# A gated cross-attention block with a spiking FFN on one core: the first batches' steps in another order, roundings moved to ScalarE, smaller gate groups

## What is computed

```python
q = layernorm(x); k = v = ctx                    # 8 heads of 32
ig, fg = gates(concat(q, k, v))                  # per token and head
cs = cumsum(log_sigmoid(fg)); log_D = masked(cs_i - cs_j + ig_j)
C = (q @ k.T / sqrt(32)) * exp(log_D - rowmax(log_D))
h = (C / max(|C.sum|, exp(-rowmax))) @ v
x1 = x + tanh(g0) * layernorm(h) * ln_scale
y = square(relu(layernorm(x1) @ W_fc.T)) @ W_proj.T       # 256 -> 1024 -> 256
n = number of spikes of y in 5 leaky integrate-and-fire steps
out = x1 + tanh(g1) * n / 5
```

## Time and profile before

| | us |
|---|---|
| median of 3 runs (lowest, highest) | 690.0 (688.1, 690.67) |
| the profiled execution | 687.64 |
| its span, first to last instruction | 685.8 |
| PE busy | 616.9 |
| DVE busy | 523.9 |
| ACT busy | 400.4 |
| POOL busy | 323.9 |

### The profile page before, as it was taken

The page is one execution under the profiler, slowest core; times in us unless marked ns, Lnnn a source line. Parts: engine busy times, 40 slices in busy tenths (PEclk is TensorE's granted clock), DMA queues, the critical chain, the costliest instruction groups (busy, mean ns, idle before and its releaser), DMA issues.

```text
span 685.8 us, 17089 instructions
## 1 busy us (share of the span) xinstructions
PE 616.9 (90%) x6064; PEld 523.6 (76%) x6064; DVE 523.9 (76%) x1218; ACT 400.4 (58%) x863; POOL 323.9 (47%) x391
## 2 busy tenths in 40 slices
PE   2355688899999999999999999999999999999975
PEld 1245677778887888888888888888888878787865
DVE  4768687897888878897979878887888696948242
ACT  4654464765747756665756674775667464644432
POOL 3566657563555274544675365527454445510000
PEclk9999899999999999999999999999999999999998
DMA  8863677674429437752692657562774065000000
GB/s 242 157 150 76 133 127 127 125 129 104 82 86 199 74 104 140 142 89 91 129 173 65 117 112 158 96 108 96 138 144 73 24 126 95 15 18 32 0 32 31
DMA packets 73171, 71.29 MB, mean 104 GB/s; under 512 B 8704, under 2 KB 68736, under 8 KB 73088
## 3 DMA queue, kind: packets, MB, share of 16 engines
q1 hardware_dynamic: 71968, 70.02, 50.2%
q10 hardware_dynamic: 1120, 0.18, 0.1%
HBM read 27.44 MB, written 8.39 MB: 52 GB/s over the span
## 4 chain that ended last, share of the span: by engine, by line
PE 75%; DVE 8%; issue 7%; ACT 4%; POOL 3%; DMA 2%; SPq 1%; DVEq 0%; POOLq 0%; ACTq 0%
PE y_ps L1007 28%; PE z_ps L971 24%; PE misc_ps L448 4%; PE qk_ps L695 4%; PE arg_ps L680 3%; PE misc_ps L514 2%; PE pv_ps L742 2%; PE pv_ps L744 2%; PE pv_ps L743 2%; PE pv_ps L819 2%; DVE pv_ps L871 1%; DVE decay L714 1%; DVE stat L345 1%; ACT relu L981 1%; ACT decay L706 1%
## 5 line engine op out<-in xcount | busy, mean ns | idle before, releaser
L724 POOL TENSOR_TENSOR c_lo<-decay 128x512 bf16<-128x512 f32 x128 | 132.7, 1042 | 153.9 <-DVE decay L714 153.7
L1007 PE MATMUL y_ps<-wpr,relu 128*128 128x256 f32 x680 | 160.8, 381 | 1.2 <-issue 1.2
L1007 PEld LDWEIGHTS y_ps<-wpr,relu 128*128 128x128 f32 x680 | 124.9, 190 | 17.2 <-issue 1.4
L971 PE MATMUL z_ps<-x_hi,wfc_hi 128*128 128x512 f32 (+1 forms) x288 | 124.9, 434 | 5.9 <-ACT relu L981 3.8
L706 ACT ACTIVATE decay<-arg_ps,lqk_col 128x512 f32<-128x512 f32 x128 | 87.3, 682 | 37.5 <-PE arg_ps L683 31.3
L971 PE MATMUL z_ps<-x_hi,wfc_lo 128*128 128x512 f32 (+1 forms) x288 | 107.4, 373 | 0.0
L971 PE MATMUL z_ps<-x_lo,wfc_hi 128*128 128x512 f32 (+1 forms) x288 | 107.2, 372 | 0.0
L714 DVE TENSOR_TENSOR decay<-qk_ps,decay 128x512 f32<-128x512 f32 x128 | 86.9, 679 | 22.3 <-PE qk_ps L695 19.9
L981 ACT ACTIVATE relu<-z_ps 128x512 f32<-128x512 f32 (+1 forms) x96 | 52.5, 547 | 73.7 <-PE z_ps L971 69.0
L1007 PE MATMUL y_ps<-wpr,w_raw 128*128 128x256 f32 x344 | 81.4, 381 | 0.0
L1007 PEld LDWEIGHTS y_ps<-wpr,w_raw 128*128 128x128 f32 x344 | 63.3, 190 | 8.1
(11 more groups left out here) (128 smaller groups left out, 1473.5 us busy)
## 6 DMA issues: line engine op xcount, KB each, us to landing
x_in<-x SPq DMA_DIRECT2D x32, 256.0 KB, 3.3
v_in<-ctx_rows SPq DMA_DIRECT2D x32, 256.0 KB, 4.2
kT_in<-ctx_cols SPq DMA_DIRECT2D x32, 256.0 KB, 4.0
k_stack<-kT_hi SPq DMA_DIRECT2D x64, 128.0 KB, 3.3
k_stack<-kT_lo SPq DMA_DIRECT2D x64, 128.0 KB, 3.9
q_stack<-qT_hi SPq DMA_DIRECT2D x64, 128.0 KB, 4.4
q_stack<-qT_lo SPq DMA_DIRECT2D x64, 128.0 KB, 4.9
out<-w_raw SPq DMA_DIRECT2D x32, 256.0 KB, 3.4
```

The source lines that it names most:

```text
L724: e.tensor_tensor(c_lo[i % NCH][:, :], c, top(c), ALU.subtract).then_inc(sem("c_lo"), 1)
L971: ins = e.matmul(z_ps[:, tokens(q)], lhsT, rhs, start=(n == 0), stop=(n == len(terms) - 1))
L1007: ins = e.matmul(y_ps[:, t, :], relu[n % NRE][:, t * P:(t + 1) * P], wpr[:, j, :], start=(j == 0 and t % ST == 0), stop=(j == FT - 1), ski ...
```

## The change

- `GROUPS`: batches 4 to 7 form two groups of two instead of one of four, so there are ten groups instead of nine.
- `k_hi` and `v_hi_step` become ACT copies; the rounding of the first weights (now `split_wfc_hi`) too, and `split_wfc_lo` stays on DVE.
- `am_rows` becomes `load_a_rows` and `load_m_rows`; for batches 0 and 1 the m rows are issued by ACT, for all others both by SP.
- All five lists and `MISC_ORDER` are written in another order. In the prologue of POOL `setup_fixed` stands ahead of `setup_pool`. The loop bodies hold the same steps for four batches and two jobs, shifted by one batch and reordered.

```diff
-    GROUPS = [(0, 1), (1, 1), (2, 2)] + [(b, 4) for b in range(4, B, 4)]
+    GROUPS = [(0, 1), (1, 1), (2, 2), (4, 2), (6, 2)] + [(b, 4) for b in range(8, B, 4)]
...
+        def split_wfc_hi(e, n):
+            e.wait_ge(sem("ld_wfc"), 16)
+            e.activation(wfc_half(wfc_hi[:, :, :], n), wfc_half(w_raw[:, :], n), ACT.Copy).then_inc(sem("wfc_hi"), 1)
+
+        def split_wfc_lo(e, n):
+            e.wait_ge(sem("wfc_hi"), n + 1)
+            e.tensor_tensor(wfc_half(wfc_lo[:, :, :], n), wfc_half(w_raw[:, :], n),
+                            wfc_half(wfc_hi[:, :, :], n).bitcast(fp32), ALU.subtract).then_inc(sem("wfc_ready"), 1)
...
-            e.tensor_scalar(kT_hi[b % NK][:, :, :], kT_in[b % NC][:, :, :], 1.0, 1.0, ALU.mult, ALU.mult).then_inc(sem("k_hi"), 1)
+            e.activation(kT_hi[b % NK][:, :, :], kT_in[b % NC][:, :, :], ACT.Copy).then_inc(sem("k_hi"), 1)
...
-            e.tensor_scalar(hi, src, 1.0, 1.0, ALU.mult, ALU.mult).then_inc(sem("v_hi"), 1)
+            e.activation(hi, src, ACT.Copy).then_inc(sem("v_hi"), 1)
...
-            for k, (rows, first) in enumerate(((a_rows, 0), (m_rows, 3))):
-                for j in range(3):
-                    e.dma_start(rows[b % NAM][first + j:first + j + 1, :, :], am_part[g % 2][row:row + NH, j, k, :])\
-                     .then_inc(sem(f"ld_am{b % NAM}"), 16)
+            for j in range(3):
+                e.dma_start(rows[b % NAM][first + j:first + j + 1, :, :], am_part[g % 2][row:row + NH, j, k, :])\
+                 .then_inc(sem(f"ld_am{b % NAM}"), 16)
...
+            load_m_rows(e, 0)
...
-            gates_out(e, 6)
-            x2_hi_step(e, 0)
```

More of the change, by code:

```diff
@@ L1395, in vector_program @@
+            h_norm(e, 0)
+            q_lo(e, 6)
+            ln2_stats(e, 0)
+            cmul(e, 1, 1)
+            x1_step(e, 0)
             gate_pre(e, 2)
-            cmul(e, 0, 3)
+            state_own(e, 1)
+            ln3_stats(e, 0)
             gate_cumsum(e, 2)
-            cmul(e, 1, 0)
-            cmul(e, 1, 1)
+            ln3_offset(e, 0)
+            cmul(e, 1, 2)
             gate_cummax(e, 2)
-            split_wfc(e, 2)
-            h_norm(e, 0)
-            q_lo(e, 5)
-            ln2_stats(e, 0)
@@ L1568, in tensor_program @@
             qk(e, 0, 1)
-            arg(e, 0, 2)
+            state(e, 0)
+            qk(e, 0, 2)
             arg(e, 0, 3)
-            state(e, 0)
-            gate_products(e, 3)
             q_T(e, 4)
-            qk(e, 0, 2)
-            gate_T(e, 2)
+            pv(e, 0, 0)
             qk(e, 0, 3)
             q_T(e, 5)
+            qk(e, 1, 0)
             arg(e, 1, 0)
+            inter(e, 0)
+            pv(e, 0, 1)
+            qk(e, 1, 1)
+            floor_T(e, 1)
+            q_T(e, 6)
@@ L1579, in tensor_program @@
             arg(e, 1, 1)
-            qk(e, 1, 0)
-            qk(e, 1, 1)
-            inter(e, 0)
-            pv(e, 0, 0)
             arg(e, 1, 2)
-            pv(e, 0, 1)
+            arg(e, 1, 3)
+            gate_products(e, 2)
+            gate_products(e, 3)
+            qk(e, 1, 2)
+            gate_T(e, 2)
+            state(e, 1)
             gate_products(e, 4)
-            floor_T(e, 2)
-            arg(e, 1, 3)
-            qk(e, 1, 2)
-            q_T(e, 6)
+            pv(e, 1, 0)
@@ L1591, in tensor_program @@
+            x2_T(e, 0)
             qk(e, 1, 3)
-            arg(e, 2, 0)
-            state(e, 1)
-            qk(e, 2, 0)
-            arg(e, 2, 1)
-            gate_products(e, 5)
-            pv(e, 1, 0)
+            z_step(e, 0, 0)
+            z_step(e, 0, 1)
             pv(e, 1, 1)
             inter(e, 1)
-            gate_products(e, 6)
+            gate_products(e, 5)
+            z_step(e, 0, 2)
+            gate_T(e, 3)
+            z_step(e, 0, 3)
+            floor_T(e, 2)
+            y_step(e, 0, 0)
@@ L1611, in tensor_program @@
+            x2_T(e, 1)
+            arg(e, 3, 1)
             state(e, 2)
[L1612 removed]
             qk(e, 3, 0)
[L1614 to L1616 removed]
+            arg(e, 3, 2)
+            qk(e, 3, 1)
             pv(e, 2, 0)
[L1618 to L1625 removed]
@@ L1626, in tensor_program @@
-            y_step(e, 0, 2)
-            z_step(e, 0, 5)
+            z_step(e, 0, 6)
+            floor_T(e, 3)
             pv(e, 2, 1)
             qk(e, 3, 2)
-            z_step(e, 0, 6)
-            floor_T(e, 3)
-            y_step(e, 0, 3)
+            inter(e, 2)
             arg(e, 3, 3)
-            z_step(e, 0, 7)
+            gate_products(e, 6)
             y_step(e, 0, 4)
             q_T(e, 8)
+            z_step(e, 0, 7)
+            arg(e, 4, 0)
+            z_step(e, 1, 0)
             qk(e, 3, 3)
+            z_step(e, 1, 1)
```

1091 lines of the change are left out of this document (508 added, 583 removed), and 6 rows, old and new, of the table order.

## The result

The changed kernel takes 695.87 us in the median of 6 runs (692.6 to 697.43), the kernel before 689.71 (688.1 to 690.77): a ratio of 1.009, 95% interval 1.0061 to 1.0118. It is slower by some 6 us, where I had forecast 4.0 us less. The profiled execution has a span of 692.7 against 685.8, 6.9 more. Three lines of its page (the slices of PE's busy time and of its granted clock, 17.3 us each), then windows by stage (columns as in the earlier trace rows): up to job 0, from job 0 to job 2, and the steady stretch from job 4 to job 6, which answers to 212.20:286.30 of before.

A forecast was written before the change was run, and what follows sets the result against it. PE was taken to bound the kernel from 136.8 us on, so only an earlier job 2 counts: 3.5 us there plus 0.5 less work behind, 4.0 off the 690.0 median, gives 686.0; own range 683 to 689, all cases 679 to 692.5.

The forecast's parts named there:

- The prologue: Up to job 0: batch 0's gates turned sooner and m rows issued by ACT start job 0 at 65.5, 10.5 us sooner.
- From job 0 to job 2: Between the first products of both jobs: moved work comes back behind job 0; job 2 chosen at 133.3, 3.5 us sooner.
- the two readings: Two estimates of job 2's start, keeping all idle time: PE's 131.6 with 5.3 us more work, DVE's 134.6 with 8.2.
- DVE's reading: Job 2's start counted from DVE's steps: net 8.2 us extra work, all idle time kept, giving 134.6.
- swallowed: Rival from job 0 to job 2: batch 0 gains at batches 1 to 3's cost; job 2 136.3 to 136.8, total 689 to 690; chance 0.2.
- The loop: Steady loop: same steps, ACT gets 8 roundings (5.0 us) per slot and POOL loses as much; costed at nothing.
- slower, the roundings on ACT: Rival in the loop: waiting roundings on ACT hold `relu_step`, stopping PE; at 0.15 us each, total 695.6; chance 0.18.
- The tail: Behind the loop: nothing left but PE's chain in the same order; 0.5 us less PE work counted behind job 2.
- One reading of the page: Profile of the kernel before: PE busy over 90% from the eighth slice to the third last, thin in the first seven.

The follow-up runs named there:

- pool_yield: The changed kernel with one more wait: in POOL's loop `k_lo(4n+8)` waits for `ln3_offset(4n+1)`, k and v roundings still on ACT; 688.35 us, 0.997 of before.
- round_pool: The changed kernel with the roundings of k and v back on POOL, each directly ahead of its subtraction; 685.7 us, ratio to before 0.9928.
- warm: `round_pool` with 108 extra products of 128 columns spread over PE's waits in the prologue; 684.4 us, ratio to before 0.9911.

## Why the prediction was wrong

**The prologue, right.** The fourth exponential of batch 0 started at 40.77 (forecast 41.2), `h_norm(0)` at 49.51 (49.1), job 0 at 65.8 (65.5). Inside the sum errors cancel. The first `arg` was 1.1 later than forecast (31.61): ACT's issues began 0.7 sooner and took 2.86 and not 2.0, so they ended about as forecast (28.28), and the rows landed some 3.3 us behind them where I had 2.4. From the first exponential to the fourth it was 8.5 and not 8.9, from there to `h_norm(0)` 8.7 and not 7.95. And that job 0 came 16.3 us behind `h_norm(0)` (forecast 16.4) is in part luck: in this stretch PE's granted clock fell to 0.53 (52.0 to 65.8), for which I had no term.

**From job 0 to job 2, the right terms and a wrong choice.** Of the two readings, PE's busy time grew by 7.4 us, not 5.3 (59.2 against 51.8, at a granted clock of 0.90 against 0.93). DVE's reading, 134.6, was the nearer; I chose 133.3, below it, "part of 14.1 idle us can take up extra work". It took up none: DVE was idle 15.5 us of 72.3, and busy 10.0 more where I had 8.2. PE's own waits grew from 9.0 to 13.1 us in the trace. Job 2 came 4.8 us later than forecast; the step that failed here is the choice of a time below DVE's reading. Job 2 needs batches 2 and 3, which the change doesn't bring forward: `cmul(2, 0)` starts at 82.19 instead of 72.54, and the extra DVE steps of batch 1 stand ahead of it. That this chain sets the start of job 2 is my reading; no run here tests it by itself. The rival *swallowed* describes this part; its 136.3 to 136.8 was still 1.3 us too early.

**The loop, wrong.** "I cost it at nothing, since PE's waits are 0.35 a slot and each engine has over 11 us to spare." The step that failed most is this one. It measured 2.0 us a slot, 8.1 us from job 4 to job 12, of the 10.9 by which the span missed its forecast (692.7 against 681.8, 4.0 less than 685.8). Spare time of an engine says nothing of where in the slot it lies; here DVE's two small steps fell on POOL's busiest run. With a wait on POOL for them the slot was 74.5 us. The loss is a cost of the order of the loop together with the missing roundings on POOL, and neither the order nor POOL's relief was in my sum as a possible cost. Two rows that would have told are in the trace of before, which I didn't weigh; here DVE's, then POOL's:

```profile
27.53 0.77 DVE L361 SCALAR_TENSOR_TENSOR off<-mv,rstd 128x4 f32<-128x4 f32 x1
...
27.08 1.14 POOL L622 TENSOR_TENSOR am_part<-am_rest,am_part 8x512 bf16<-8x512 f32 x1 [0.32 <-ACT am_part L620]
```

`ln1_offset(2)` took 0.77 us and ended with POOL's `am_split`, where its like take 0.15. In the loop of before, the steps at 230.1, 233.8 and 248.7 fall where POOL is idle and take 0.13 to 0.16 us.

**The rival *slower, the roundings on ACT*** gave 695.6 us, and 695.9 was measured, but as worked out it isn't what happened. ACT's copies held no relu in the changed kernel: with them left on ACT one wait on POOL gave back 7.5 us. What still separates `pool_yield` from `round_pool` (0.997 against 0.9928) may be theirs; no run shows it. In the order of before the same move did cost what the rival says, in its own way (a copy that waits for its buffer holds ACT), 20 us.

**The tail**, costed at nothing but 0.5 us less work, gave 3.1 us.

**One reading of the page** was loose: PE is busy over 90% from the ninth slice on; the eighth is an 8. Nothing in the sum hangs on it.

## What to carry to other kernels

Where two engines meet at the SBUF, look at the small steps, not at the large ones: a DVE step of 0.15 us with its operands in SBUF took up to 1.7 us in this loop (and 2.14 once, at 34.42) when it fell beside back-to-back tensor_tensor on POOL, and a chain through it is late by that. Taking work off POOL can make this worse: with the roundings on POOL two such steps took 0.86 us, with them gone 2.48. One wait on POOL for the small step gave back 7.5 us, most of the 10.2 that moving the 64 roundings back gave. And a delay put in on purpose is a test of a lead only if nothing else changes with it: look at the granted clock and PE's busy time behind it before you read where the end went.

## What was not expected of the hardware

Beside POOL's tensor_tensor a small DVE operation in SBUF either ran at once (0.16 us) or ended with a POOL operation (1.1 us), by turns, while POOL's operations kept their 1.15 us. Three issues of a small DMA from ACT took 2.86 us in one place and 1.97 in another (one of the six 1.54 us, their median 0.63), and ACT did nothing else in it. The granted clock was 1.2 GHz from about 53 to 73 us in the changed kernel, where PE had been busy 20.75 of the first 52 us, and from 74.6 to 81.5 us in the kernel before; with 108 more products of 128 columns in PE's waits it was 0.93 between 52 and 76 us. The row of the granted clock is not always complete: in `pool_yield` it says 1.00 from 52 to 76 us, yet the products of one `z_step` of job 0 there start 0.21 us apart, as in the changed kernel at its 1.2 GHz, and 0.12 apart in `warm`.
